# A mixture-of-experts block on one core: the first and the routing stages written in another order

## What is computed

```
x = x + layernorm(attention(layernorm(x)))
x = x + layernorm(ffn(layernorm(x)))

attention, per batch, 16 heads n with K = 8:
  p = x @ proj[n];  out[n] = (p @ metric[n]) @ p.T @ p        # no softmax
  result = concat(out) @ mixer_w.T + mixer_b
ffn, per token, E = 8 experts with M = 256, two chosen:
  logits = x @ gate_w.T;  idx = top_k(logits + beta, 2);  c = sigmoid(logits[idx])
  result = sum over idx of c * (silu(x @ wg[e]) * (x @ wu[e])) @ wd[e]
         + (silu(x @ sg) * (x @ su)) @ sd                     # shared expert
```

## Time and profile before

| what | value |
|---|---|
| median of 3 runs | 303.22 us (303.21 to 303.67) |
| the profiled execution, its own time | 304.09 us |
| its span, first to last instruction | 302.3 us |
| mean granted TensorE clock over the span | 0.891 |
| TensorE busy | 243.4 us (81%) |
| GpSimd busy | 184.1 us (61%) |
| VectorE busy | 175.5 us (58%) |
| ScalarE busy | 149.7 us (50%) |

### The profile page before, as it was taken

The page is one execution under the profiler, slowest core; times in us unless marked ns, Lnnn a source line. Parts: engine busy times, 40 slices in busy tenths (PEclk is TensorE's granted clock), DMA queues, the critical chain, the costliest instruction groups (busy, mean ns, idle before and its releaser), DMA issues.

```text
span 302.3 us, 6800 instructions
## 1 busy us (share of the span) xinstructions
PE 243.4 (81%) x1425; PEld 195.5 (65%) x1426; DVE 175.5 (58%) x710; ACT 149.7 (50%) x537; POOL 184.1 (61%) x243
## 2 busy tenths in 40 slices
PE   0797369997986988993349999999999999988740
PEld 0795166885774866882238887888888888863210
DVE  3773768877667677547014555556555555530592
ACT  1884417666565585441114555555555555520460
POOL 5884222887888787877402666656666576670590
PEclk9999857998998897578558999999999999999795
DMA  7790000111111111112240333323223233116952
GB/s 199 232 323 25 0 0 0 39 45 46 48 45 36 45 45 45 47 54 82 82 92 27 88 90 85 92 80 85 83 73 94 74 81 89 54 30 183 351 195 104
DMA packets 28089, 26.34 MB, mean 87 GB/s; under 512 B 6904, under 2 KB 21893, under 8 KB 28066
## 3 DMA queue, kind: packets, MB, share of 16 engines
q1 hardware_dynamic: 20736, 17.07, 19.4%
q0 software_dynamic: 4384, 8.60, 8.5%
q10 hardware_dynamic: 2946, 0.41, 0.8%
HBM read 14.83 MB, written 11.75 MB: 88 GB/s over the span
## 4 chain that ended last, share of the span: by engine, by line
PE 49%; POOL 18%; DVE 9%; issue 9%; DMA 5%; ACT 5%; SPq 1%; ACTq 1%; POOLq 1%; DVEq 0%
PE bank L1047 12%; POOL expert_rows L523 10%; PE bank L1029 7%; PE bank L1039 6%; PE bank L1031 6%; PE bank L1030 6%; POOL rstd L505 4%; PE bank L1141 3%; PE bank L998 2%; DMA xnT<-expert_results 2%; PE bank L1121 2%; POOL rstd L537 2%; DVE st L734 1%; POOL vpe L503 1%; DMA X<-n_L_attn_in_sequence_bwc 1%
## 5 line engine op out<-in xcount | busy, mean ns | idle before, releaser
L554 POOL DMA_INDIRECT expert_results<-eo,rowt x72 | 70.4, 978 | 53.9 <-issue 29.3
L523 POOL DMA_INDIRECT expert_rows<-src,slot x64 | 63.7, 995 | 18.2 <-issue 17.3
L793 DVE TENSOR_TENSOR hid<-sgate,bank 128x256 f32<-128x256 f32 x104 | 43.5, 419 | 51.5 <-ACT sgate L573 51.3
L573 ACT ACTIVATE sgate<-bank 128x256 f32<-128x256 f32 x104 | 40.0, 385 | 61.3 <-PE bank L1031 60.9
L1047 PE MATMUL bank<-down,hidT 128*128 (+1 forms) x416 | 68.4, 290 | 0.4 <-ACT ysh L648 0.4
L1047 PEld LDWEIGHTS bank<-down,hidT 128*128 128x128 f32 x416 | 58.5, 203 | 2.0 <-ACT ysh L648 1.0
L1039 PE MATMUL bank<-ident,hid 128*128 128x128 f32 x208 | 42.6, 288 | 14.9 <-DVE hid L793 14.2
L1039 PEld LDWEIGHTS bank<-ident,hid 128*128 128x128 f32 x208 | 27.4, 148 | 30.6 <-DVE hid L793 18.7
L580 ACT ACTIVATE hidT<-bank 128x256 f32<-128x256 f32 x104 | 40.4, 389 | 12.7 <-PE bank L1039 11.6
L1029 PE MATMUL bank<-gu_hi,rh 128*128 x72 | 35.4, 492 | 2.0 <-DVE rl L937 1.4
L1031 PE MATMUL bank<-gu_hi,rl 128*128 x72 | 29.1, 404 | 0.0
(11 more groups left out here) (166 smaller groups left out, 452.2 us busy)
## 6 DMA issues: line engine op xcount, KB each, us to landing
rowt<-expert_rows SPq DMA_DIRECT2D x72, 66.0 KB, 1.9
X<-n_L_attn_in_sequence_bwc SPq DMA_DIRECT2D x8, 256.0 KB, 5.6
X<-expert_results SPq DMA_DIRECT2D x8, 256.0 KB, 6.0
xnT<-expert_results SPq DMA_DIRECT2D x8, 256.0 KB, 6.6
out<-X SPq DMA_DIRECT2D x8, 256.0 KB, 2.5
expert_results<-eo,rowt POOLq DMA_INDIRECT x72, 2.2
gu_f<-in_L_ffn_gate_proj_w SPq DMA_DIRECT2D x1, 1024.0 KB, 5.7
gu_f<-in_L_ffn_up_proj_w SPq DMA_DIRECT2D x1, 1024.0 KB, 8.7
```

The lines of the kernel that those rows point to most:

```text
L523: nc.gpsimd.indirect_dma_start(rows_d, bass.IndirectOffsetOnAxis(ap=slot[u][:, i, k:k + 1], axis=0), src[u][:, k, i, :], None).then_inc(ro ...
L554: nc.gpsimd.indirect_dma_start(res_d, bass.IndirectOffsetOnAxis(ap=rowt[v][:, P:P + 1].bitcast(U32), axis=0), eo[v % 4][:], None, bounds_c ...
L573: nc.scalar.activation(sgate[v][:], gu_ps[v][:, 0:M], ACT.Silu).then_inc(silu_done, 1)
L793: nc.vector.tensor_tensor(hid[v][:], sgate[v][:], gu_ps[v][:, M:2 * M], ALU.mult).then_inc(hid_done, 1)
```

## The change

It rewrites everything ahead of the expert stage.

- The steps are batch 0 first: step s is group s % 4 of batch s // 4. The chain of batch 0 is run after its four steps, mixed with the steps of batch 1; attention of steps 0 and 1 comes between the last Gram matmuls.
- Attention gives tokens on partitions at once: two bias matmuls of 512 columns over one row (fp32r) and four fp32 matmuls of 128 columns. The transposed copy L655 and the transposes L1071 go.
- The router's rows are written by VectorE straight into `src`; TensorE transposes them from there (`rows_T`), ScalarE copies the transposes in f32 (`xT_copy`), and four fp32 matmuls of 8 columns give the logits. The fp32r parts L679 and L807, the bias matmul and the 16 small ones go; beta comes by a DMA onto all partitions and is added by VectorE (`lgb`).
- The shared expert works on the transposed rows of a whole step: per step four fp32 matmuls of 512 columns, two silu of 128 x 512, two products, eight fp32 matmuls of 128 columns, one copy. Its transposes go.
- `src` and `slot` have four buffers in place of two. ScalarE makes one copy of the rows (`second_rows`) in place of two.
- The hardware loops of this stage are written out; there is one order per engine, printed below.
- The additions of eps ahead of the inverse roots move from GpSimd to VectorE (`variance2` and the last instruction of `stats1`), the centring of `down` moves from VectorE to ScalarE, expert by expert (`centre_down`), all pads and the empty rows are sent by SyncE, and `eo` has 12 buffers, so its wait for a store goes.

The diff, cut to the orders and to the new functions. Of those it calls, `gram(s)` is the four Gram matmuls and four transposes of a step, `link` one matmul of the chain, `stats1` and `residual` the instructions of `stats` and of the x1 part of `attn_step`, `choose`, `places`, `prefix`, `high`, `low` and `make_tables` are as before apart from `lgb`.

```diff
+    SRC = 4
+    SENT = 16 * G * TOPK
...
+            for s in range(STEPS):
+                sp.dma_start(tiles(X, s), tiles(x_v, s)).then_inc(x_in[s], 16)
...
+            sp.wait_ge(route_consts, 1)
+            sp.dma_start(rows_d[EMPTY_REGION:EMPTY_REGION + P, :], empty_row[:]).then_inc(empty_out, 16)
+            pad_at = [sp.alloc_register(f"pad_at{e}") for e in range(E)]
+            sp.wait_ge(pad_ready, 1)
+            sp.reg_load(pad_at, pad_row[0:1, 0:E])
+            for e in range(E):
+                row = sp.snap(pad_at[e], min_val=0, max_val=EMPTY_REGION)
+                sp.dma_start(rows_d[bass.ds(row, P), :], empty_row[:]).then_inc(pads_out, 16)
...
+            def ln1(s):
+                gp.wait_ge(mv1_done, s + 1)
+                nc.gpsimd.tensor_scalar(nmean1[:, s, :], mv1[:, s, :, 0], -1.0, None, ALU.mult)
+                gp.wait_ge(vpe1_done, s + 1)
+                link(nc.gpsimd.tensor_tensor(rstd1[:, s, :], vpe1[:, s, :], mhalf[:], ALU.pow))
+                nc.gpsimd.tensor_tensor(shift1[:, s, :], nmean1[:, s, :], rstd1[:, s, :],
+                                        ALU.mult).then_inc(ln1_done, 1)
+            for s in range(QS):
+                ln1(s)
+            gp.wait_ge(metric_in, 16 * K)
+            nc.gpsimd.tensor_tensor(ubig[:].rearrange("p (h k) -> p h k", h=H),
+                                    bc(ucomp[:], 1, [P, H, K]), headmask[:], ALU.mult).then_inc(metric_ready, 1)
+            link(nc.gpsimd.tensor_scalar(iddiag[:], ident[:], dcomp[:], None, ALU.mult))
+            gp.wait_ge(metric_ready, 1)
+            nc.gpsimd.tensor_tensor(udiag[:], ubig[:], iddiag[:], ALU.add).then_inc(metric_ready, 1)
+            for s in range(QS, STEPS):
+                ln1(s)
...
+            def power2(i):
+                gp.wait_ge(vpe2_done, i + 1)
+                after(gp, x1_done, (i - 1) * G)
+                nc.gpsimd.tensor_tensor(rstd2[i % 2][:], vpe2[i % 2][:], mhalf[:], ALU.pow).then_inc(rstd2_done, 1)
+            def power3(i):
+                gp.wait_ge(vpe3_done, i + 1)
+                after(gp, xt_done, (i - 1) * G)
+                nc.gpsimd.tensor_tensor(rstd3[i % 2][:], vpe3[i % 2][:], mhalf[:], ALU.pow).then_inc(rstd3_done, 1)
...
+            power2(0)
+            rest_of_constants()
+            power3(0)
+            power2(1)
+            power3(1)
+            for i in range(STEPS):
+                gp.wait_ge(src_x_done, i + 1)
+                gp.wait_ge(src_done, i + 1)
+                scatter(i, 0, 1)
+                if 0 < i < STEPS - 1:
+                    power3(i + 1)
+                scatter(i, 1, 5)
+                if i + 2 < STEPS:
+                    power2(i + 2)
+                scatter(i, 5, 8)
...
-            act.dma_start(beta_sb[:], beta.rearrange("(a e) -> a e", a=1)).then_inc(router_w_in, 16)
+            act.dma_start(beta_bc[:], bc(beta, 0, [P, E])).then_inc(router_w_in, 16)
...
+            def centre_down(e, n):
+                for a in range(MC):
+                    last = nc.scalar.activation(down_junk[:, a, :], down[:, e, a, :], ACT.Copy, scale=-1.0 / C,
+                                                accum_out=down_nmean[:, e, a:a + 1])
+                last.then_inc(down_c, 1)
+                act.wait_ge(down_c, 2 * n + 1)
+                for a in range(MC):
+                    last = nc.scalar.activation(down[:, e, a, :], down[:, e, a, :], ACT.Identity,
+                                                bias=down_nmean[:, e, a:a + 1])
+                last.then_inc(down_c, 1)
+            for s in range(QS):
+                normalise(s, 0, G)
+                if s == 1:
+                    weights()
+            gram_copy(0)
+            normalise(4, 0, 2)
+            chain_copy(0, 1, T1)
+            normalise(4, 2, G)
+            LT_copy()
+            normalise(5, 0, 2)
+            chain_copy(0, 3, R_sb)
+            normalise(5, 2, G)
+            chain_copy(0, 4, A_sb)
+            normalise(6, 0, G)
+            squares(0)
+            normalise(7, 0, G)
+            squares(1)
+            gram_copy(1)
+            chain_copy(1, 1, T1)
+            act.wait_ge(shared_in, 48)
+            centre_down(E, 0)
+            chain_copy(1, 3, R_sb)
+            chain_copy(1, 4, A_sb)
+            for i in range(STEPS + 1):
+                if i < STEPS:
+                    xT_copy(i)
+                    tanh(i)
+                    second_rows(i)
+                    silu(i, 0)
+                    silu(i, 1)
+                if i > 0:
+                    ysh_copy(i - 1)
+                if i + 2 < STEPS:
+                    squares(i + 2)
+                if i < STEPS:
+                    if i == 0:
+                        act.wait_ge(gu_in, 32)
+                        act.wait_ge(down_in, 16 * E)
+                    high(i)
+                    centre_down(i, i + 1)
...
+            stats1(0)
+            stats1(1)
+            stats1(2)
+            xnT_copy(0)
+            stats1(3)
+            xnT_copy(1)
+            dve.wait_ge(bias_ready, 1)
+            nc.vector.tensor_tensor(bias_lo[:], bc(bias_ps, 1, [1, G, C]), bias_hi[:].bitcast(F32),
+                                    ALU.subtract).then_inc(bias_ready, 1)
+            xnT_copy(2)
+            stats1(4)
+            xnT_copy(3)
+            dve.wait_ge(metric_ready, 2)
+            dve.wait_ge(ubigT_mm, 1)
+            nc.vector.tensor_tensor(metric[:], ubigT_ps, udiag[:], ALU.add).then_inc(metric_ready, 1)
+            stats1(5)
+            head_blocks(0)
+            stats1(6)
+            stats1(7)
+            xnT_copy(4)
+            xnT_copy(5)
...
+            variance2(0)
+            residual(0)
+            xnT_copy(6)
+            xnT_copy(7)
+            head_blocks(1)
+            for i in range(STEPS + 1):
+                if i < STEPS:
+                    normalise(i)
+                if i + 1 < STEPS:
+                    variance2(i + 1)
+                if i == 0:
+                    residual(1)
+                    dve.wait_ge(router_w_in, 32)
+                    dve.wait_ge(route_consts, 1)
+                if i > 0:
+                    for a in range(MC):
+                        hidden(i - 1, a)
+                    low(i - 1)
+                if i < STEPS:
+                    choose(i)
+                    places(i)
+                if i == STEPS - 1:
+                    make_tables()
+                if i > 0 and i + 1 < STEPS:
+                    residual(i + 1)
...
+            def attention(i):
+                b = i // QS
+                if i == 0:
+                    pe.wait_ge(bias_ready, 2)
+                if i % QS == 0:
+                    pe.wait_ge(chain_sb[b], 5)
+                pe.wait_ge(xnT_done, i + 1)
+                after(pe, x1_done, i * G)
+                for part in (bias_hi, bias_lo):
+                    mm(attn_ps[:, :], ones_r[:], part[:].rearrange("a i c -> a (i c)"), start=part is bias_hi,
+                       stop=False, skip_group_check=True)
+                for n in range(G):
+                    at = (i % QS * G + n) * P
+                    last = mm(attn_ps[:, n * P:(n + 1) * P], xnT[:, b, at:at + P], A_sb[b][:], start=False, stop=True,
+                              skip_group_check=True)
+                last.then_inc(attn_mm, 1)
+            weights()
+            gram(0)
+            gram(1)
+            gram(2)
+            metric_T()
+            gram(3)
+            link(0, 1, S_sb[0][:], Wf)
+            metric_W()
+            link(0, 2, Wf, T1[0][:])
+            gram(4)
+            link(0, 3, Gm[0][:], mixT[:])
+            pe.wait_ge(LT_sb, 1)
+            link(0, 4, LT[:], R_sb[0][:])
+            gram(5)
+            attention(0)
+            gram(6)
+            attention(1)
+            gram(7)
+            link(1, 1, S_sb[1][:], Wf)
+            link(1, 2, Wf, T1[1][:])
+            link(1, 3, Gm[1][:], mixT[:])
+            link(1, 4, LT[:], R_sb[1][:])
...
+            def rows_T(i):
+                for n in range(G):
+                    pe.wait_ge(xt_done, i * G + n + 1)
+                    if n == 0:
+                        after(pe, xT_sb, i)
+                    last = nc.tensor.transpose(xT_ps[:, n * P:(n + 1) * P], src[i % SRC][:, 0, n, 0:P], ident[:])
+                last.then_inc(xT_tr, 1)
+            def logits(i):
+                pe.wait_ge(xT_sb, i + 1)
+                after(pe, place_c, i * 3)
+                for n in range(G):
+                    last = mm(lg_ps[:, n, :], xT[i % 2][:, n * P:(n + 1) * P], gwT[:], start=True, stop=True)
+                last.then_inc(logits_mm, 1)
...
+            def shared(i, a):
+                if i == 0 and a == 0:
+                    pe.wait_ge(shared_in, 48)
+                    pe.wait_ge(xnT_done, STEPS)
+                if i == 0 and a == 1:
+                    for b in range(B):
+                        pe.wait_ge(chain_sb[b], 5)
```

(30 more changed lines are left out.)

969 lines of the change are left out of this document (357 added, 612 removed).

## The result

The changed kernel takes 307.81 us (median of four runs, 306.18 to 309.38), the kernel before 303.22 (302.29 to 303.67): a ratio of 1.0155, 95% interval 1.0096 to 1.0215. It is slower, by 4.6 us. The profiled execution took 307.4 us with a span of 305.5, where before it took 304.09 with 302.3.

A forecast was written before the change was run, and what follows sets the result against it. GpSimd's scatters decide the first 154 us before, TensorE the expert stage; after, a 13.5 us step. Last scatter +5.6, handover -1.1: +4.5 on 304.09, 308.6, as median 307.7 us; range 296.5 to 313, the forecast's own 303.9 to 311.

The forecast's parts named there:

- First scatter: GpSimd's first scatter starts at 50.2 us, 2.9 us earlier than before; bounds 46.5 and 54.
- The ring without the clock: One step's path through ScalarE, TensorE and the choice, `xT_copy` to next `xT_copy`, sums to 12.3 us without clock penalty.
- GpSimd alone: Scatters and inverse roots without pauses take 92.9 us, 12.3 us per step of eight scatters and two inverse roots.
- The price of half clock: After TensorE's pause, logits and most of `shared(i,0)` run at half clock: +1.2 us, a step of 13.5.
- 0.50 at the logits of most steps: Expected sign: TensorE's granted clock is 0.50 when it does the logits in most steps.
- the transpose rule: Transposes don't count as busy for TensorE's clock, so 3.9 us are one pause; if they did, step nearer 12.3.
- The pause: TensorE has only four short transposes for 3.9 us per step, from the end of attention(i+2) to logits(i+1).
- The last scatter's end: GpSimd's last scatter ends at 153.7 us instead of 148.09: +5.6.
- The handover: Behind the last scatter, SyncE's 1.1 us wait for the empty rows goes, with all pads sent early: -1.1 us.
- The faster case: Clock kept or ScalarE's part of the ring shorter, GpSimd never idle: 294.9 us, deciding at step 12.85; chance 0.27.
- Half clock for twice as long in each step: TensorE at half clock over two stretches per step: step 15.2 us, total 320 us; chance 0.07.
- `vpe` ahead of `power3`: Expected sign: GpSimd waits for VectorE's `vpe` ahead of `power3`; forecast wait of GpSimd 1.2 us in each step.

The follow-up runs named there:

- a4: Changed kernel plus 20 unused bf16 matmuls on TensorE between `rows_T` and `logits`; 319.6 us, ratio 0.952 to the kernel before on the same chip.
- a1: Changed kernel with ScalarE's `xT_copy(i + 1)` moved ahead of `high` and `centre_down`; 320.5 us, ratio 0.958 to the kernel before on the same chip.
- a2: Changed kernel with attention ahead of `shared_down` and ScalarE's `ysh_copy` behind `centre_down`; 319.9 us, ratio 0.956 to the kernel before on the same chip.
- b2: Changed kernel plus two unused 128x512 copies on ScalarE behind `second_rows(i)`, in its wait; 334.4 us, ratio 0.986 to the kernel before on the same chip.
- a3: Changed kernel with both new orders, attention ahead of `shared_down` and `xT_copy` ahead of `high`; 318.5 us, ratio 0.952 to the kernel before on the same chip.
- c1: Changed kernel with the orders of a3 and b5 together; 297.3 us, ratio 0.985 to the kernel before on the same chip.
- b3: Changed kernel with VectorE's `stats1(3)` moved ahead of `xnT_copy(0)` in the first stage; 332.1 us, ratio 0.979 to the kernel before on the same chip.
- b5: Changed kernel with `stats1(3)` and `stats1(4)` ahead of `xnT_copy(0)` and `stats1(5)` behind it; 307.5 us, ratio 1.0155 to the kernel before on the same chip.
- b1: Changed kernel plus two unused 128x512 copies on ScalarE behind `centre_down`, ahead of `xT_copy`; 338.6 us, ratio 0.997 to the kernel before on the same chip.
- c0: The changed kernel measured once more, with no edit; 308.1 us, ratio 1.0186 to the kernel before on the same chip.
- b4: The kernel before with all eight pads sent by SyncE, measured twice; 338.6 us, ratio 0.989, and 338.5 us, ratio 0.9965, to the kernel before.

## Why the prediction was right

- **First scatter** at 50.2: measured 50.48. Its chain held: TensorE started at 10.98 behind the transfer of `beta_bc` (11 was taken), attention(0) started its bias matmuls at 29.89 and those with `A_sb` at 30.54 (30.5), and `stats1(3)` came behind the first copy, at 15.63.
- **The ring without the clock**, 12.3: a4 gives 12.40 at a clock of 1.00. a1 and a2 each shorten it at a different engine and get the same, and b2 shows that the same engine's time outside it is free. The ring is shown. Its terms were near, but not all for the same reason. From start to start in the step of a4 above: copy to logits 0.63 (0.7 taken), logits to the choice 1.41 (1.21), choice 1.82 (2.1), `prefix` 0.14 (0.2), `shared(i,1)` 1.80 (1.72), `shared_down` 1.88 (1.8), attention to `squares` 1.85 (1.65), `squares` 1.02 (1.12), `high` 0.52 (0.62), `centre_down` 1.33 (1.2, bounds 1.0 and 1.65). They add up to 12.40; errors of up to 0.3 us of both signs cancelled, which is luck.
- **GpSimd alone**, 12.3: a3 and c1 run at 12.26 and 12.25. The prediction's own terms give a little less than it wrote, 92.7 us for the stage and 12.1 per step (8 x 1.26 + 2 x 1.03).
- **The price of half clock**, +1.2: 13.39 less 12.40 is 1.0. The position was off: the prediction expected 0.50 at the logits and most of `shared(i,0)`. In the usual step the logits are at 1.00, and the last part of `shared(i,0)` with the first part of `shared(i,1)` is slow, so the sign "0.50 at the logits of most steps" did not come. What was expected occurred in step 1 of the changed kernel, in two steps each of b3 and b5 and in most of b1, and where it hits a later step it costs 2.3 us more than the usual one. The price is therefore right in mechanism, near in size, and was reasoned for matmuls other than those that paid it; that 1.0 is so near to 1.2 is in part luck. On the transpose rule the prediction weighed from the Trainium skill (TensorE: Matmul & The Clock Gate, Part 4): the transposes fell directly behind attention (94.13 against its end at 94.29) and not inside the pause, so no run here tests it.
- **The pause**, 3.9: from the end of attention (94.29) to the logits (97.83) it is 3.5, of which the transposes fill 0.4.
- **The last scatter's end**, 153.7: 152.18. The seven distances sum to 91.70 instead of 93.7, of which the very first is 1.0 (12.54; by the code it has no `shared_down`, which is 1.9 us, and the 6.8 us at half clock in step 1 took part of that back), the five middle ones 0.5 and the last, which lacks attention and squares, 0.5 (12.20 instead of 12.7); the start gives +0.28 and the last eight scatters +0.2.
- **The handover**, -1.1: -1.07, and for the reason named.
- **The total**: +4.5 was expected on the profiled execution and +3.3 was measured (307.4 against 304.09). The median, 307.81, agrees with 307.7 better than its terms do: this profiled run lay 0.4 us below its own median, where that of before lay 0.9 above. That agreement to 0.1 us is luck.
- **The rivals.** The faster case needed a step under 12.85; a1, a2, a3 and a4 are that case, made on purpose, and c1 at 297.3 us shows that its reckoning was sound. It was one order of instructions away. Half clock for twice as long in each step did not come; it came in step 1, and in most steps of b1, whose pause is longer.

The predicted sign `vpe` ahead of `power3` was seen, but only as a follower of the ring, as a3 shows.

## What to carry to other kernels

When a schedule is tightened from lagged loops to one step at a time, walk the ring once round through every engine, and look for work in it that nobody in the ring waits for. Here two weight preparations of 1.9 us stood ahead of a copy of 0.6, and the order of these instructions was worth 1.1 us in each middle step and 6.9 us over all seven (a1), more than the 4.6 us by which the change made the kernel slower. A pause of TensorE is paid twice when it has no slack behind it, once as itself and once as half clock on what follows; with slack it is not paid at all, so make the slack first and don't chase the clock. And a wait that ends in a fixed order often only moves: ask what stands behind the next instruction of that engine, as b3 and b5 show.

## What the runs showed of the hardware

- After pauses of the same 3.1 us, half clock lasted about 3.4 us from a point 1.4 to 2.3 us behind the start of the logits in most steps. It lasted about 6.8 us, from inside the pause, in step 1 of the changed kernel, c0, b2 and b5 and in one later step of b3 and of b5, and in step 1 of b3 from 0.4 us behind the start of the logits. The same program has both, so a forecast of such a kernel needs a spread of some 2.3 us per step that is so hit.
- Which of the two a step gets followed a pattern in these traces. In the changed kernel the fall came 1.64, 1.77, 1.90, 2.03 and 2.17 us behind the start of the logits of steps 2 to 6, some 0.13 us later each time. In b5 it came 1.89, 2.02, 2.15 and 2.29 us behind it and then, in the step of 15.67 us, 1.0 us ahead of it. In b3 it came 2.24 behind it and then 1.0 ahead, in the step of 15.63. No run was made to test this.
- Twenty bf16 matmuls of 256 columns, 2.35 us in all, in a pause of 2.8 us kept the clock at 1.00 for 67 us. The Trainium skill (TensorE: Matmul & The Clock Gate, Loop structure matters more than you think) advises to order the loop so that TensorE has no long waits; a4, in which the wait is filled, agrees on the clock, while a3 shows that in this kernel the order pays through the ring and not through the clock.
- On the chips of three of the groups the kernel before took 336 to 341 us instead of 302 to 303 (medians), with engines waiting for nothing that the profile shows (in a3 TensorE's weight loads once for 9.96 us ahead of L1023, up to 147.96, and ScalarE for 10.2 us over the same time). Most steps of the changed order were the same there; the order of the kernel before, seen in the two b4 runs, had steps of 14.9 us instead of 12.6 and one of over 18. What holds the engines up on such chips was not looked into.
